# A hybrid layer on one Trainium2 core: attention's output projection from high and low parts in three matmuls

## The reference

```python
def _L0_attn_a_ref(x, Wqkv, bqkv, Wo, bo):          # 16 heads of 32 channels
    kqv = x @ Wqkv + bqkv                            # split into q, k, v
    scores = jnp.einsum('bsnh,btnh->bnst', k, q) / math.sqrt(HEAD_SIZE)
    scores = jnp.triu(scores) + -10000.0 * jnp.tril(ones, k=-1)
    attn = jax.nn.softmax(scores, axis=2)
    out = jnp.einsum('bnkq,bknh->bqnh', attn, v)
    return out.reshape(b, s, 512) @ Wo + bo
x = x + _L0_attn_a_ref(_layernorm(x), ...)
```

## Time and profile before

| | us |
|---|---|
| runs of the kernel before | 3270.25, 3282.86, 3271.09; median 3271.09 |
| the profiled execution, its own time | 3254.58 |
| its span, first to last instruction | 3253.0 |
| PE busy in it | 3014.0 (93%) |
| DVE busy | 2205.5 (68%) |
| ACT busy | 1096.9 (34%) |
| POOL busy | 761.4 (23%) |
| mean granted clock of PE | 0.962 of full |

### The profile page before, as it was taken

The page is one execution under the profiler, slowest core; times in us unless marked ns, Lnnn a source line. Parts: engine busy times, 40 slices in busy tenths (PEclk is TensorE's granted clock), DMA queues, the critical chain, the costliest instruction groups (busy, mean ns, idle before and its releaser), DMA issues.

```text
span 3253.0 us, 59676 instructions
## 1 busy us (share of the span) xinstructions
PE 3014.0 (93%) x20772; PEld 2069.4 (64%) x20772; DVE 2205.5 (68%) x2975; ACT 1096.9 (34%) x1733; POOL 761.4 (23%) x1071
## 2 busy tenths in 40 slices
PE   3589999999999998999989999999999999999998
PEld 3445457777755446777765444777776454677776
DVE  1356667777656667777775666777766566687777
ACT  1223414444213333343412332443431333244342
POOL 3121111333221111233312110133330211123332
PEclk7799999999989999999999999999999999999999
DMA  7422102111231211111122220111112311021112
GB/s 232 157 51 66 46 14 65 49 46 36 67 86 46 65 27 46 51 45 50 50 75 60 51 65 20 53 45 51 45 44 86 72 45 46 14 73 46 50 45 75
DMA packets 161189, 191.57 MB, mean 59 GB/s; under 512 B 43962, under 2 KB 103994, under 8 KB 159226
## 3 DMA queue, kind: packets, MB, share of 16 engines
q1 hardware_dynamic: 157150, 175.83, 19.5%
q0 software_dynamic: 2720, 10.49, 0.8%
q10 hardware_dynamic: 1152, 3.15, 0.5%
HBM read 106.99 MB, written 23.36 MB: 40 GB/s over the span
## 4 chain that ended last, share of the span: by engine, by line
PE 75%; DVE 11%; issue 4%; DMA 4%; SPq 3%; ACT 2%; POOL 1%; ACTq 0%; DVEq 0%; POOLq 0%
PE ps L723 13%; PE ps L725 12%; PE ps L724 12%; PE ps L875 7%; PE ps L838 5%; PE ps L858 5%; PE ps L1056 4%; PE ps L942 3%; PE ps L1042 2%; PE ps L1102 2%; DVE LM L1660 2%; PE ps L1065 2%; DMA KS<-EV 1%; DVE mneg L1567 1%; PE ps L733 1%
## 5 line engine op out<-in xcount | busy, mean ns | idle before, releaser
L723 PE MATMUL ps<-uh,win 128*128 128x512 f32 x1536 | 630.8, 411 | 4.9 <-POOL win L1820 4.3
L725 PE MATMUL ps<-uh,win 128*128 128x512 f32 x1536 | 605.3, 394 | 0.0
L724 PE MATMUL ps<-ul,win 128*128 128x512 f32 x1536 | 602.4, 392 | 0.0
L1567 DVE TENSOR_REDUCE mneg<-ps 128x1 f32<-128x128 f32 (+7 forms) x512 | 362.0, 752 | 146.1 <-PE ps L841 142.9
L1239 ACT ACTIVATE PR<-ps 128x1024 f32<-128x1024 f32 (+3 forms) x384 | 310.5, 810 | 406.6 <-PE ps L861 270.0
L723 PEld LDWEIGHTS ps<-uh,win 128*128 128x128 f32 x1536 | 290.9, 189 | 96.6 <-issue 29.6
L875 PE MATMUL ps<-PR,VG 128*32 128x512 f32 (+3 forms) x1536 | 336.3, 514 | 12.5 <-DVE OS L1573 8.3
L877 PE MATMUL ps<-PR,ones 128*32 128x512 f32 (+3 forms) x1536 | 336.3, 514 | 0.0
L1684 DVE TENSOR_TENSOR LM<-ps,LM 128x512 f32<-128x512 f32 x256 | 170.1, 686 | 243.2 <-PE ps L1056 197.2
L725 PEld LDWEIGHTS ps<-uh,win 128*128 128x128 f32 x1536 | 290.3, 189 | 66.0
L724 PEld LDWEIGHTS ps<-ul,win 128*128 128x128 f32 x1536 | 291.5, 190 | 54.9
(11 more groups left out here) (220 smaller groups left out, 5140.7 us busy)
## 6 DMA issues: line engine op xcount, KB each, us to landing
raw<-in_t SPq DMA_DIRECT2D x128, 256.0 KB, 2.7
QS<-EV SPq DMA_DIRECT2D x192, 128.0 KB, 2.4
KS<-EV SPq DMA_DIRECT2D x168, 128.0 KB, 2.4
X<-in_L_attn_b_W_in_dram SPq DMA_DIRECT2D x10, 1024.0 KB, 7.8
in_t<-tiles POOLq DMA_DIRECT2D x10, 1024.0 KB, 8.4
XN<-in_L_attn_a_x_dram SPq DMA_DIRECT2D x40, 256.0 KB, 4.7
win_raw<-in_L_attn_a_Wqkv_dram SPq DMA_DIRECT2D x34, 256.0 KB, 3.3
win_raw<-in_t SPq DMA_DIRECT2D x32, 256.0 KB, 2.7
```

The lines of the kernel that those rows point to most:

```text
L723: pe.matmul(dst, hi_l, hi_r, start=first, stop=False)
L724: pe.matmul(dst, hi_l, lo_r, start=False, stop=False)
L725: return pe.matmul(dst, lo_l, hi_r, start=False, stop=last)
L1567: dve.tensor_reduce(mneg[:, hh, t:t + 1], wide(b0)[:, 0:(t + 1) * P], AX.X, ALU.max, negate=True).then_inc(a_max.sem, 1)
```

## The change

The output projection uses `three` on four new F32R pairs: `woh_a` and `wol_a` (weights), `OTh` and `OTl` (attention's output). ACT casts the high parts, DVE subtracts the low ones.

- `woh_a` and `wol_a`, 8 KB each, take the room of V; `OTl` takes that of QS and KS of half 0; `OTh` that of the EV tiles.
- In the last group, half 0 (p = 6), behind the exponential of unit 1, ACT waits for the weights' transfer and for `vg_done` of `p + 1` (POOL's last copy out of V), and casts all of `wo`. DVE subtracts behind the maxima of unit 5.
- In half 1 (p = 7), ACT casts the six half slices of `OT` for k = 0 to 2 behind the exponentials of units 4 to 9; DVE subtracts them in units 5 to 10. The two half slices of k = 3 follow behind the loops.
- PE waits for `wo_lo` and `ot_lo` in place of `s_wo` and `o_scaled`.

```diff
+            with ExitStack() as c2:
+                woh_a = sb("woh_a", [P, KT, D], F32R, at=c2)
+                wol_a = sb("wol_a", [P, KT, D], F32R, at=c2)
             V = sb("V", [P, TT, D], at=c)
...
             second = head_rows(1)
+            with ExitStack() as c2:
+                OTl = sb("OTl", [P, GROUPS, L], F32R, at=c2)
             rows_of = [head_rows(0), second]
             QS, KS = ([rows_of[i][w] for i in range(2)] for w in range(2))
+            with ExitStack() as c2:
+                OTh = sb("OTh", [P, GROUPS, L], F32R, at=c2)
             EV = [[sb(f"EV{w}{i}", [P, L], F32R, at=c) for i in range(2)] for w in range(2)]
...
-                pe.wait_ge(s_wo, b * 16 + 16)
+                wo_lo.wait(pe, b, 1)
                 row_product(lambda dst, k, t0, first, end:
-                            pe.matmul(dst, OT[:, k, t0:t0 + P], wo[:, k, :], start=first, stop=end),
-                            b * 2, lambda: o_scaled.wait(pe, b * 8 + 5, 2), lambda: o_scaled.wait(pe, b * 8 + 7, 2))
+                            three(dst, OTh[:, k, t0:t0 + P], OTl[:, k, t0:t0 + P], woh_a[:, k, :], wol_a[:, k, :], first, end),
+                            b * 2, lambda: ot_lo.wait(pe, b, 2 * GROUPS - 2), lambda: ot_lo.wait(pe, b, 2 * GROUPS))
...
+                def output_hi(k, c):
+
+                    cols = slice(c * HB, (c + 1) * HB)
+                    o_scaled.wait(act, b * 8 + 2 * k + 1, c + 1)
+                    act.copy(OTh[:, k, cols], OT[:, k, cols]).then_inc(ot_hi.sem, 1)
...
+                                if hf == 0 and last and u == 1:
+                                    act.wait_ge(s_wo, b * 16 + 16)
+                                    vg_done.wait(act, p + 1, 1)
+                                    act.copy(woh_a[:, :, :], wo[:, :, :]).then_inc(wo_hi.sem, 1)
+                                if hf == 1 and last and u >= 4 and u < 4 + 2 * (GROUPS - 1):
+                                    output_hi((u - 4) // 2, u % 2)
...
+                for c in range(2):
+                    output_hi(GROUPS - 1, c)
                 experts(b * 4 + 1, b * 2)
...
+                def output_lo(k, c):
+
+                    cols = slice(c * HB, (c + 1) * HB)
+                    ot_hi.wait(dve, b, 2 * k + c + 1)
+                    dve.tensor_tensor(OTl[:, k, cols], OT[:, k, cols], OTh[:, k, cols].bitcast(F32), ALU.subtract).then_inc(ot_lo.sem, 1)
...
+                                if hf == 0 and last and u == 5:
+                                    wo_hi.wait(dve, b, 1)
+                                    dve.tensor_tensor(wol_a[:, :, :], wo[:, :, :], woh_a[:, :, :].bitcast(F32), ALU.subtract).then_inc(wo_lo.sem, 1)
+                                if hf == 1 and last and u >= 5 and u < 5 + 2 * (GROUPS - 1):
+                                    output_lo((u - 5) // 2, (u - 5) % 2)
...
+                for c in range(2):
+                    output_lo(GROUPS - 1, c)
                 dve.wait_ge(s_bias, b + 1)
```

More of the change, by code:

```diff
@@ L260, in hybrid_layer @@
         o_scaled = signal("o_scaled", 2)
+        wo_hi = signal("wo_hi", 1)
+        wo_lo = signal("wo_lo", 1)
+        ot_hi = signal("ot_hi", 2 * GROUPS)
+        ot_lo = signal("ot_lo", 2 * GROUPS)
         z_pe = signal("z_pe", TT)
@@ L336, in hybrid_layer @@
         SIGNALS_OF = {
-            "vector": [wout_lo, bcw_lo, ln_var, ln_xh, ln_lo, v_done, w_add, pj_lo, a_max, o_copied, o_rec, z_dve, g_in, g_w, u_add,
+            "vector": [wo_lo, ot_lo, wout_lo, bcw_lo, ln_var, ln_xh, ln_lo, v_done, w_add, pj_lo, a_max, o_copied, o_rec, z_dve, g_in, g_w, u_add,
                        al_dve, a_dve, cm_dve, cm_low, ed_in, xz_dve, bc_dve, scan, m_dve, y_mid, y_dve, gate],
-            "scalar": [wout_hi, wv_hi, qkw_hi, xzw_hi, bcw_hi, ln_hi, pj_hi, m_act, ex, g_exp, t_act, sp_act, dc_act, xz_act, xt_act, bc_act,
+            "scalar": [wo_hi, ot_hi, wout_hi, wv_hi, qkw_hi, xzw_hi, bcw_hi, ln_hi, pj_hi, m_act, ex, g_exp, t_act, sp_act, dc_act, xz_act, xt_act, bc_act,
                        bt_act, cm_act, ed_act, ds_act, dt_act, seg_act],
```

## The result

The changed kernel takes 3284.6 us (median of 20 runs), the kernel before 3269.07 (20 runs). The ratio is 1.0045 with a 95% interval of 1.0023 to 1.0067: slower by some 15 us (7.5 to 22 by the interval). One of the 20 runs of the changed kernel, 3319.33 us, was a slow one and is left out of the ratio. The forecast was +15.8 us on 3271.09, so 3287, with the move "just at the bound of what can be told". Both hold: the time moved the forecast way, and by a hair less than 0.5%.

The account below looks back on a forecast made before the run. PE, busy for 93% of the span, was taken as the bound. Per batch -5.16 + 5.5 + 2.9 + 0.6 + 0.1 = +3.94 us, times four +15.8, giving 3287 us on the median of 3271.09; range 3268 to 3307.

Parts of the forecast that it names:

- The product: Output projection on PE: 96 F32R matmuls at 233 ns replace 32 fp32 ones, 22.4 us for 27.57, gaining 5.16 a batch.
- The page's rate: Output projection: F32R matmuls run at the fp32 passes' 215 ns, gain 6.9 us a batch, 3280 us; chance 0.02.
- The wait behind V: p = 6 behind unit 1: ACT waits for POOL's last copy out of V, delaying PE's weigh(2); +5.5 us a batch.
- The clock: PE after its hole in p = 6 comes back at half rate; +2.9 us a batch, bounds 0 and 5.8.
- a longer low stretch: PE's clock after the hole: a drop twice as long, 2.9 us more a batch, 3298 us; chance 0.13.
- near the row: PE after the hole in p = 6: one clock drop costs about the 2.98 us seen going into p = 5, batch 1.
- The subtraction: DVE subtracts the weights behind unit 5's maxima in p = 6, delaying PE's transpose of the maxima; +0.6 us a batch.
- Casts of the outputs: ACT's casts and DVE's subtractions of attention's output in p = 7 fit into gaps; +0.1 us a batch, bounds 0 and 0.8.
- The sum: Whole kernel: all terms give +3.94 us a batch, +15.8 us in four batches, 3287 us on the median.
- ACT's wait costs nothing: p = 6: ACT's wait for V is hidden, leaving product, subtraction and casts; -17.8 us, 3253 us; chance 0.08.
- No price of the clock: p = 6: PE's hole costs its length but its clock stays up; +4.2 us, 3275 us; chance 0.12.
- The faster rival: Another name for "ACT's wait costs nothing": the wait in p = 6 is hidden, 3253 us; chance 0.08.

Follow-up runs that it names:

- the wait alone: Kernel before plus only ACT's wait behind unit 1 of p = 6 for POOL's last copy out of V, product in fp32; 3298.15 us, ratio 1.0095.
- the first experiment: Changed kernel with the weights' cast moved behind unit 5 and their subtraction behind unit 10 of p = 6; 3269.25 us, ratio 1.0002 against the kernel before.
- the filled hole: Changed kernel with 24 unused 128x512 matmuls on PE before weigh(2) of p = 6; 3272.4 us, ratio 1.0014 against the kernel before.
- third experiment: Changed kernel with only the weights' subtraction moved, behind unit 10 of p = 6, cast still behind unit 1; 3293.65 us, ratio 1.0065 against the kernel before.

## Why the prediction was right, point by point

- **The product**: forecast 22.4 us and a gain of 5.16; measured 21.92 and 5.65. The mechanism held: 96 F32R matmuls took less time than 32 fp32 ones (27.57 us), without a hole, with their operands ready in time. The F32R stream ran at 21.92 / 96 = 228 ns a matmul, faster than the 233 ns of the earlier trace rows, slower than 215 ns, a quarter of an fp32 matmul. The page's rate (the Trainium skill, TensorE: Matmul & The Clock Gate, "Phases on the wall clock", 216 ns) was not reached here either; at 216 ns the gain would be 27.57 - 96 x 0.216 = 6.8 us, not the 6.9 that I wrote, an estimate either way. Why the same helper runs at 228 in one product and 233 in another is open.
- **The wait behind V**: forecast ACT held 5.6 us, PE 5.6 late, price 5.5; measured 5.61 idle on ACT, 5.38 on PE, and 5.5 us of delay against the last slice of p = 5. Right, and the run of the wait alone shows it as the cause.
- **The clock**: forecast 2.9 us, bounds 0 and 5.8; measured 4.4, in every batch. Right in kind, but the measured price is one and a half times the forecast, and lies midway between it and the 5.8 of "a longer low stretch". The step that was mis-sized is "near the row, since unit 3 and what follows are the same work one half later". The row came from a place where the clock fell after a shallow bubble. There the low clock lasted 4 x 2 x (0.06 + 0.50 + 0.30) = 6.9 us (the clock is at 0.50 when low, so low time is twice the missing share), with PE busy in nearly all of it. Behind the real hole it lasted 4 x 2 x (0.39 + 0.50 + 0.50 + 0.32) = 13.7 us, twice as long; 3.5 us of that fell into the hole, and some 10 us over work, longer than the "next 4 to 8 us". In the run of the wait alone it was some 11.7 us over work. Price by time worked at the low clock: 2.98 / 6.9, 4.4 / 10.2 and 5.0 / 11.7, 0.43 each, as an estimate from one batch of each; the fall in p = 7 of the first experiment was cheaper, 5.6 us for some 17. The slices of p = 6 therefore came 10.1 us later, not the 8 to 9 forecast. Why the low clock lasts longer in one place than in another is open.
- **The subtraction**: forecast 0.6; the filled hole and the cast behind unit 5 leave 0.2 each for cast and subtraction together. DVE's idle time took more of it than I worked out; my own rows leave less than 0.6 too, 2.28 - 0.94 - 0.97 = 0.37.
- **Casts of the outputs**: forecast 0.1; measured nothing, 21.04 us from p = 6's first slice to the product in batch 0 of both kernels. The six casts stand in ACT's gaps, and the last slice was ready before PE asked. One thing I hadn't seen: DVE's subtractions there slow POOL's slices to 1.72 us, which nobody waits for.
- **The sum**: forecast +3.94 us a batch, measured +4.4 by the traces. The product's extra 0.5 us and the 0.5 us too much for subtraction and casts paid for most of the clock's 1.5 us. That the forecast of +15.8 us met the medians' +15.5 is thus in part luck: two errors cancelled, and the interval is 14 us wide.
- **The rivals**: "ACT's wait costs nothing" is refuted by the wait alone. "No price of the clock" is what the filled hole shows, 3272.4 us against my 3275. "A longer low stretch" came true by half: the low clock lasted twice as long as in its row, but a quarter of it cost nothing, since PE stood still, so the price stayed at 4.4 of the 5.8 us. In two batches of the cast behind unit 2 the price was well above 5.8. The faster rival's 3253 us is what a move of one cast reaches and passes.

## What to carry to other kernels

When a new tile takes the room of an old one, look up when the old tile's last reader ends, and put the wait for it at a point of each in-order engine's program that comes later; here four units later turned +15 us into -29. Count a hole on PE at its length plus a fall of the clock (3.4 to 5.1 us in 14 of 16 batches with holes of 3.7 to 5.4 us here, 8.6 and 11 in the other two), and judge such moves by a distance inside one trace rather than by the span. Moving DVE's work needs a look at POOL too, not only at DVE's own gaps.

## What the runs showed of the hardware

- A subtraction on DVE of two SBUF tiles (2.28 us) beside a multiplication on POOL stretches the latter from 1.29 to 3.25 us, in eight of eight cases (first and third experiment); DVE's own time didn't change. Against a shorter subtraction of outputs POOL's slice took 1.72 us. DVE's maxima, which read PSUM, leave POOL's slice at 1.28 us. The Trainium skill (GPSIMD Engine Reference, "Specifications") says that POOL shares its SBUF interfaces with VectorE and contends with instructions that have two SBUF inputs; the traces agree, and in all eight cases POOL was the one that waited: the subtraction had started 0.15 us before it, and POOL's slice ended 1.1 us behind the subtraction's end. No run shows what happens when POOL starts first.
- After the hole PE's clock came back only after some 10 us of work in the changed kernel, and after some 20 and 27 us in two batches with the cast behind unit 2. With 24 matmuls in the hole it didn't fall there in any of the four batches. The Trainium skill (TensorE: Matmul & The Clock Gate, Part 1) has activity release the throttle; these traces agree that idling brings the clock down, but "busy" by the profile wasn't enough to bring it back soon.
